# Eight-product visits give way to seven-product ones in the second of three sweeps, and GpSimd makes one block difference for four columns

## The reference

```python
h = relu(layernorm(x))
T1 = adj @ h                        # sweep 1
T2 = 2 * (adj @ T1) - h             # sweep 2
T3 = 2 * (adj @ T2) - T1            # sweep 3
x = x + h @ w[0] + T1 @ w[1] + T2 @ w[2] + T3 @ w[3] + bias
h = expmap(relu(layernorm(x)))      # a scale for each row
x = x + logmap(adj @ h) @ kernel + bias
```

## Time and profile before

| | before |
|---|---|
| median of three executions | 1759.46 us (1758.67 to 1760.33) |
| the profiled execution | 1758.64 us |
| span of its instructions | 1756.7 us |
| TensorE busy | 1708.7 us (97%) |
| DVE busy | 1285.4 us (73%) |
| ScalarE, GpSimd busy | 266.6 us (15%), 164.3 us (9%) |
| DMA | 665.13 MB, mean 379 GB/s |
| second sweep | about 690 to 1080 us |

### The profile page before, as it was taken

The page is one execution under the profiler, slowest core; times in us unless marked ns, Lnnn a source line. Parts: engine busy times, 40 slices in busy tenths (PEclk is TensorE's granted clock), DMA queues, the critical chain, the costliest instruction groups (busy, mean ns, idle before and its releaser), DMA issues.

```text
span 1756.7 us, 66856 instructions
## 1 busy us (share of the span) xinstructions
PE 1708.7 (97%) x30828; PEld 1018.2 (58%) x30828; DVE 1285.4 (73%) x2081; ACT 266.6 (15%) x507; POOL 164.3 (9%) x228
## 2 busy tenths in 40 slices
PE   7999999999999999999999999999999999999997
PEld 5655555555655555555555555566655555656554
DVE  7157777776878687789889886487778776776745
ACT  1013222111111011011100001222110111010014
POOL 0000000000000010211011000111001000000003
PEclk9999999999999999999999999999999999999999
DMA  9999999999999987889999987799999999999996
GB/s 368 420 420 418 419 418 415 414 414 411 403 409 406 397 304 287 334 317 332 340 338 334 339 326 277 273 386 398 411 419 410 406 420 415 418 419 412 419 419 263
DMA packets 95013, 665.13 MB, mean 379 GB/s; under 512 B 11408, under 2 KB 13712, under 8 KB 14608
## 3 DMA queue, kind: packets, MB, share of 16 engines
q1 hardware_dynamic: 93744, 660.64, 94.1%
q10 hardware_dynamic: 992, 0.23, 0.1%
HBM read 658.74 MB, written 2.10 MB: 376 GB/s over the span
## 4 chain that ended last, share of the span: by engine, by line
PE 79%; DMA 12%; DVE 6%; issue 1%; ACT 1%; SPq 1%; POOL 0%; DVEq 0%; ACTq 0%
PE own_bank L788 22%; PE row_bank L788 18%; DMA ring<-adj_blocks 12%; PE work_bank L690 12%; PE row_bank L690 9%; PE work_bank L788 7%; PE turned L690 5%; PE turned L703 2%; DVE ring L1069 1%; PE row_bank L826 1%; PE work_bank L804 1%; PE own_bank L690 1%; DVE ring L1073 1%; PE own_bank L804 1%; PE row_bank L804 0%
## 5 line engine op out<-in xcount | busy, mean ns | idle before, releaser
L1069 DVE TENSOR_TENSOR ring<-ring 128x1024 f32<-128x1024 f32 x323 | 401.8, 1244 | 130.0 <-DMA ring<-adj_blocks 64.1
L788 PE MATMUL own_bank<-ring 128*32 128x256 f32 x5024 | 432.8, 379 | 0.2
L788 PE MATMUL own_bank<-ring,nodes 128*32 128x256 f32 x3768 | 384.2, 379 | 1.3 <-DVE ring L1069 1.1
L788 PE MATMUL row_bank<-ring 128*32 128x256 f32 x3488 | 300.2, 379 | 0.0
L788 PEld LDWEIGHTS own_bank<-ring 128*32 128x32 f32 x5024 | 230.9, 110 | 108.5 <-DVE ring L1073 1.7
L690 PE MATMUL row_bank<-ring,nodes 128*32 128x256 f32 (+1 forms) x3856 | 263.9, 382 | 17.4 <-DMA ring<-adj_blocks 16.1
L788 PE MATMUL row_bank<-ring,nodes 128*32 128x256 f32 x2616 | 266.3, 379 | 3.6 <-POOL ring L649 1.9
L690 PE MATMUL work_bank<-ring,nodes 128*32 128x256 f32 x4288 | 252.4, 380 | 4.8 <-issue 3.1
L1075 DVE TENSOR_TENSOR ring<-ring 128x512 f32<-128x512 f32 x323 | 230.2, 713 | 11.0
L788 PEld LDWEIGHTS own_bank<-ring,nodes 128*32 128x32 f32 x3768 | 189.4, 110 | 83.6 <-DVE ring L1069 4.5
L1073 DVE TENSOR_TENSOR ring<-ring 128x512 f32<-128x512 f32 x323 | 229.1, 709 | 11.1
(11 more groups left out here) (159 smaller groups left out, 1154.0 us busy)
## 6 DMA issues: line engine op xcount, KB each, us to landing
ring<-adj_blocks SPq DMA_DIRECT2D x626, 1024.0 KB, 10.5
out<-resid SPq DMA_DIRECT2D x16, 128.0 KB, 2.9
resid<-x SPq DMA_DIRECT2D x7, 256.0 KB, 12.0
resid<-x SPq DMA_DIRECT2D x2, 128.0 KB, 3.4
w_raw<-cheb_weight ACTq DMA_DIRECT2D x2, 64.0 KB, 9.1
bias<-cheb_bias ACTq DMA_DIRECT2D x1, 32.0 KB, 3.1
bias<-hyp_bias ACTq DMA_DIRECT2D x1, 32.0 KB, 5.1
w_raw<-hyp_kernel ACTq DMA_DIRECT2D x2, 16.0 KB, 9.8
```

What stands on the lines that cost most here:

```text
L788: done = nc.tensor.matmul(bank[lane:lane + H, columns], left(a, h, level), right[b][:, h, :], start=first and k < 2, stop=k == 6, tile_pos ...
L1069: nc.vector.tensor_tensor(first_two(n, block), block[:, :, N2].rearrange("p (k h) n -> p k h n", k=2), block[:, 0:2, :].rearrange("p h (k ...
```

## The change

Column 13 of rows 11 to 0 gets a seven-product visit like all the others; the eight-product code, its work bank and its addition in the JOIN go. For the columns 10 to 13 of the second sweep T4 is made by GpSimd instead of DVE: it waits for T2 (`s_mixed`), subtracts, and raises a semaphore of its own, for which TensorE waits ahead of the sixth round. In GpSimd's program a T4 stands at the step two visits ahead, like DVE's differences, and so ahead of that step's SUMS or BIAS and behind those of earlier steps. The counting of `s_mixed` follows (two or three for a visit). The cut diff:

```diff
-PLAIN_COLUMN = NB - 3
+POOL_COLUMNS = range(NB - 6, NB - 2)
...
-    plain = [i for i in fast if phase_of[i] == 1 and steps[i][2] == PLAIN_COLUMN]
-    fast = [i for i in fast if i not in plain]
+    fourth_no = {i: n + 1 for n, i in enumerate(i for i in fast if phase_of[i] == 1 and steps[i][2] in POOL_COLUMNS)}
     mix_no = {i: n for n, i in enumerate(fast)}
-    mix_before = {}
+    mix_before, mixed_before = {}, {}
     for i in fast:
+        mixed_before[i] = sum(2 if j in fourth_no else 3 for j in fast[:mix_no[i]])
...
-            for s in steps:
+            for i, s in enumerate(steps):
+                for j in mix_before.get(i, []):
+                    if j in fourth_no:
+                        block = ring[:, slot_of[load_of[j]], :, :]
+                        pool.wait_ge(s_mixed, mixed_before[j] + 2)
+                        nc.gpsimd.tensor_tensor(mix_of(mix_no[j], 2), block[:, 2:4, N1], mix_of(mix_no[j], 1), ALU.subtract)\
+                            .then_inc(s_fourth, 1)
                 if s[0] == "BIAS":
...
-                        if k in (1, 3, 5):
-                            pe.wait_ge(s_mixed, 3 * n + (k + 1) // 2)
+                        if k == 5 and i in fourth_no:
+                            pe.wait_ge(s_fourth, fourth_no[i])
+                        elif k in (1, 3, 5):
+                            pe.wait_ge(s_mixed, mixed_before[i] + (k + 1) // 2)
...
-                if i in plain:
-                    low, high = pairs[group_of[i]]
-                    bank = work_banks[work_bank[i]]
...
-                    dve.wait_ge(s_mixed, 3 * n + 2)
-                    nc.vector.tensor_tensor(mix_of(n, 2), block[:, 2:4, N1], mix_of(n, 1), ALU.subtract).then_inc(s_mixed, 1)
+                    if j not in fourth_no:
+                        dve.wait_ge(s_mixed, mixed_before[j] + 2)
+                        nc.vector.tensor_tensor(mix_of(n, 2), block[:, 2:4, N1], mix_of(n, 1), ALU.subtract).then_inc(s_mixed, 1)
...
-                    if group in plain_bank:
-                        step(nc.vector.tensor_tensor(joined[:, N2], both, aside[:, N2], ALU.add))
-                        extra = work_banks[plain_bank[group]]
-                        nc.vector.tensor_tensor(joined[:, N2], joined[:, N2], extra[:, N2], ALU.add)
-                    else:
-                        nc.vector.tensor_tensor(joined[:, N2], both, aside[:, N2], ALU.add)
+                    nc.vector.tensor_tensor(joined[:, N2], both, aside[:, N2], ALU.add)
```

More of the change, by code:

```diff
@@ L365, in chebyshev_hyperbolic_kernel @@
             pair_before = spill_no[i]
-        elif kind == "AGAIN" or kind == "OWN" and s[1] >= FAST_FROM or i in plain or \
+        elif kind == "AGAIN" or kind == "OWN" and s[1] >= FAST_FROM or \
                 kind == "BOTH" and phase_of[i] == 0 and i not in group_of:
@@ L375, in chebyshev_hyperbolic_kernel @@
                 bank_before[i] = bank_user[bank]
-            bank_user[bank] = ("OWN", i, s[1]) if kind == "OWN" else ("PLAIN", i, group_of[i]) if i in plain else \
-                ("SPILL", i, spill_no[i])
-            if kind == "OWN" or i in plain:
+            bank_user[bank] = ("OWN", i, s[1]) if kind == "OWN" else ("SPILL", i, spill_no[i])
+            if kind == "OWN":
                 held_until[bank] = steps.index(("JOIN", s[1], phase_of[i] + 1, 0))
@@ L408, in chebyshev_hyperbolic_kernel @@
     loads = len(slot_of)
-    plain_bank = {group_of[i]: work_bank[i] for i in plain}
     first_of_row, last_of_row = {}, {}
@@ L543, in chebyshev_hyperbolic_kernel @@
         s_mixed = sem("block_mixed")
+        s_fourth = sem("fourth_difference_by_pool")
         s_aside = sem("halves_exchanged")
@@ L791, in _ @@
                     done.then_inc(s_visit, 1)
-                if i in plain:
-                    low, high = pairs[group_of[i]]
-                    bank = work_banks[work_bank[i]]
[L796 to L810, removed]
+                if kind == "BOTH" and phase_of[i] > 0 and i not in mix_no:
                     level = phase_of[i] + 1
@@ L1071, in _ @@
                         .then_inc(s_mixed, 1)
-                    dve.wait_ge(s_mixed, 3 * n + 1)
+                    dve.wait_ge(s_mixed, mixed_before[j] + 1)
                     nc.vector.tensor_tensor(mix_of(n, 1), block[:, 2:4, N2], mix_of(n, 0), ALU.subtract).then_inc(s_mixed, 1)
-                    dve.wait_ge(s_mixed, 3 * n + 2)
-                    nc.vector.tensor_tensor(mix_of(n, 2), block[:, 2:4, N1], mix_of(n, 1), ALU.subtract).then_inc(s_mixed, 1)
+                    if j not in fourth_no:
+                        dve.wait_ge(s_mixed, mixed_before[j] + 2)
+                        nc.vector.tensor_tensor(mix_of(n, 2), block[:, 2:4, N1], mix_of(n, 1), ALU.subtract).then_inc(s_mixed, 1)
                 if kind == "BOTH" and phase_of[i] == 0 and i not in group_of:
```

## The result

The changed kernel takes 1809.07 us, the median of six executions (1807.65 to 1812.58); the kernel before takes 1759.34 (1758.40 to 1760.33, six). The ratio is 1.0286, 95% interval 1.0276 to 1.0296: 49.7 us slower. The forecast was 1799.5, slower by 40, in a range of 1772 to 1822.

The account below looks back on a forecast made before the run. TensorE was taken to bound the second sweep; row losses of 0.5 (row 11), 3.9 (row 10), 32.9 (rows 9 to 2) and 3.3 us (rows 1, 0) summed to 40.6, giving 1799.5 us, range 1772 to 1822.

Parts of the forecast that it names:

- What bounds the kernel: Second sweep: TensorE, busy 387.15 of 390 us, sets the pace; a microsecond lost there shifts all that follows by one.
- the lost cover: Column 13: the eight-product visit (3.45 us) hid the JOIN, which leaves DVE 6.48 us past the row's start.
- The first stall: Column 13: TensorE waits 0.83 us for DVE's first difference (L1069 before, L1059 after), made behind the JOIN.
- Two engines exclude each other: DVE and GpSimd differences block each other: column 13's T4 some 2.2 us, 1.28 alone; DVE's next about 1.7, not 0.69.
- The second stall: Column 13, sixth round: TensorE waits 1.28 us for GpSimd's T4, held by DVE's difference for column 12.
- The queue of GpSimd: Column 10's T4 stands behind the previous row's SUMS and BIAS, making TensorE wait 2.44 us in rows 9 to 2.
- the walk: One full row followed from T0, the preceding row's last-visit end, and applied to others: 1.67 + 2.44 us in rows 9 to 2.
- (c): Rival: T4 costs 1.84 us, 15 us more, 1815; a falling clock would add, only row 10's wait near; chance 0.12.
- the third stall: Column 10, sixth round: TensorE waits 2.44 us for GpSimd's T4 in rows 9 to 2, not in rows 1 and 0.
- (a): Rival: GpSimd's work is free beside DVE, 0.75 us lost in each of 11 rows, 1766.5 us; chance 0.08.
- (b): Rival: column 13's L1069 and T4 come in time, so the 5.2 us saved come in, 1753.5 us; chance 0.05.
- (d): Rival: GpSimd's queue doesn't hold column 10, only 21 us stay, 1780 us; chance 0.10.

Follow-up runs that it names:

- e4: Changed kernel with GpSimd writing zeros by a memset that reads nothing in place of T4, the fourth difference left out: 1765.71 us, ratio 1.0033.
- e5: Changed kernel with SUMS and BIAS of rows 10 to 0 placed behind column 10's T4 in GpSimd's program: 1792.57 us, ratio 1.0189.
- e3: Changed kernel with column 10's T4 back on DVE, columns 11 to 13 still on GpSimd: 1786.44 us, ratio 1.0154.
- e2: Kernel before, eight-product visits kept, with T4 of columns 10 to 12 made by GpSimd: 1764.84 us, ratio 1.0031.
- e9: Changed kernel with unread filler products ahead of TensorE's waits for column 10's T4 (rows 9 to 2) and row 10's wait for SUMS: 1803.79 us, ratio 1.0252.
- e1: Changed kernel without GpSimd's part: seven-product visits, all differences on DVE: 1771.68 us, ratio 1.0068.
- e8: As e7, but eight-product visits kept in rows 11 to 6: 1758.22 us, ratio 0.9997 against the kernel before.
- e6: As e7, but row 10 keeps its eight-product visit: 1762.49 us, ratio 1.0022 against the kernel before.
- e7: As e1, with the JOIN's last two operations put off behind column 13's differences: 1767.98 us, ratio 1.0053 against the kernel before.

## Why the prediction was right, and where it was short

**What bounds the kernel, and the lost cover: right.** TensorE waited for next to nothing before (2.9 us), and each wait added came through to the end: 52.8 us in the sweep's rows, none given back. The first stall was walked as 0.83 us, and the trace shows 0.85 in that place; in all eleven rows it is 0.83 to 1.10.

**Two engines exclude each other: right.** T4 of column 13: 2.2 us forecast, 2.17 measured; alone 1.28 and 1.28; L1063 behind it about 1.7, measured 1.63. Carrying 0.46 and 0.73 us on to 1.28 was exact. The second stall, forecast as 1.28, is 1.04 us, because TensorE comes to it later (2 below). e4 shows that signals, dispatch and writes have no part in it. Here the rule of the Trainium skill (SBUF — State Buffer, Who interferes with whom) is borne out on both its sides: a GpSimd instruction that only writes is not held by a DVE instruction with two inputs in SBUF.

**The queue of GpSimd: right.** 2.44 us forecast, 2.30 measured in seven rows, 8 to 2, and not in rows 1 and 0. For row 9 the walk doesn't hold: column 10 is its last visit, so TensorE first waits there for SUMS, 0.56 us, and then 0.98 for T4. e5 shows that the queue makes it.

**The sizes that were short.** 40.6 us forecast, 52.8 in the profiled execution, 49.7 in the medians. Two terms:

1. *The clock*, 9.0 us of the 52.8. The prediction had it in rival (c), tied to row 10's wait alone. The step that failed is that sentence, "only row 10's wait of 4 us comes near": behind the third stall, of 2.3 us, the clock fell in four of seven rows, 1.6 us each, and row 10's fall cost 2.9. Even row 10's was put at nothing in the sum. e3 shows that the first two stalls alone don't do it, e2 that a wait of 2.61 us can do it with no other idle time near, e9 what it costs.
2. *Restarting*, 0.2 us for each wait, put at nothing. The 16 entries (two rounds) behind a T4 wait took 1.11 us in the chain, where two rounds take 0.86; the 48 behind e1's wait for L1059 took 2.80, where six rounds take 2.59. The row periods, read from DVE, say the same: 0.84 + 0.2 - 0.43 makes the 0.6 of e4, 0.32 + 0.2 the 0.5 of e2, 0.84 + 1.05 + 0.4 - 0.43 the 1.9 of e3. That products are issued before the ones ahead have ended (in the timeline entries of 0.38 us start 0.21 us apart), and a wait breaks that, is the likely reason; no run tests it. In a full row 0.85 + 1.04 + 2.30 us idle, 3 x 0.2 for the restarts, less 0.43, make the 4.4 of e9. The walk's 0.83 + 1.28 + 2.44 - 0.43 = 4.1 counted from the ends of products, as the chain gives them. Over the rows that is some 3 us.

The two make up the 12.2 us. That row 9 adds nothing is luck. The prediction took it for a full row, 4.1 us; it isn't one, and e9 without the filler's 1.4 us loses 4.2 there, by 1.75 us of waiting for SUMS in place of the third stall.

**The rivals.** (a), free work beside DVE, falls by T4's 2.17 us. (b), faster, falls by L1059 at 6.03 us past T0. (c), a T4 of 1.84 us, falls by 1.28, though the clock named in it came. (d), a queue that doesn't hold column 10, falls by the seven waits of 2.30 us; e3 is what it would have looked like, 1786.

**In the experiments** I was right on e2 and e4 to 2 us and on e8. e9 came out 2 us above what I expected, with a filler that didn't fit in row 9. I was wrong on e1, e3, e5, e6 and e7 by 5 to 12 us, mainly for one reason: I walked a long row and multiplied, and the short rows 10 to 7 have a bound of their own. Falls of the clock in them, in row 9 of e5 and row 10 of e7, came on top.

## What to carry to other kernels

An operation that is slower, and looks like slack, may be the cover for something else: before a visit is made shorter, ask what the engine beside it does in that time, and walk one period of both from the last point at which they meet. Walk the shortest period too, not only the typical one, since the fixed work in it (here the JOIN, the turn, the sums) weighs most there. Moving a two-input elementwise operation from DVE to GpSimd doesn't relieve DVE while both have work: here it cost the next DVE operation 0.94 us to save 0.6 to 0.7.

## What the hardware showed beyond that

A fall of the clock can be bought off: 1.7 us of products that nobody reads, in a wait of 2.3 us, keep TensorE at 2.4 GHz and save 1.6 us a row. They have to fit in the wait: where it had shrunk, they cost 1.4 us.

The length of one idle time didn't tell whether the granted clock falls to 0.50. Behind 2.30 us, with 0.85 and 1.04 us some 13 and 10 us ahead of it, it fell in four of seven alike rows, for 3.4 us each time. Behind 2.61 us, with none ahead of it, it fell for 3.4 (e2). With 3.91 us it fell for 6.8 (changed kernel, e3, e5), with 4.05 us for 6.8 in e5 and not at all in e1, with 5.06 for 6.8 (e7). Behind idle times up to 2.05 us it never fell in this sweep.

And each wait of TensorE costs 0.2 us more than its idle time, for waits from 0.3 to 2.3 us.
